# Routed experts of a perceiver block: GpSimd rounds with a one-tensor operation, VectorE waits later for split weights, and the last up product moves behind an output

## Chip, cores and metric

The kernel runs on one core of one Trainium2 chip. The metric is the device time of one execution in microseconds (us); the median of three runs stands for a kernel.

## The reference

The function takes `x` (16 x 64 tokens of 512 features) and a context (16 x 1601 x 512). It adds a cross attention over the context, then a relative-position self attention, then a block with latent attention and a mixture of experts. Only the last part is touched:

```
def moe(xn, Wg_s, Wu_s, Wd_s, Wg_r, Wu_r, Wd_r, W_router, routing_bias):
    shared = silu(xt @ Wg_s) * (xt @ Wu_s) @ Wd_s
    probs = jax.nn.sigmoid(xt @ W_router + routing_bias)
    scores, idx = jax.lax.top_k(probs, TOPK)             # TOPK = 2 of ER = 7
    scores = scores / jnp.sum(scores, axis=-1, keepdims=True)
    wts = jnp.sum(jax.nn.one_hot(idx, ER) * scores[..., None], axis=1)
    g = jnp.einsum('th,ehi->tei', xt, Wg_r)
    u = jnp.einsum('th,ehi->tei', xt, Wu_r)
    combined = jnp.einsum('tei,eih,te->th', silu(g) * u, Wd_r, wts)
    return shared + combined
```

All 1,024 tokens go to a shared expert and each to two of seven routed ones. Every weight matrix is 512 x 512, in float32.

## The kernel before

**Precision.** A float32 product is made of three products in the type fp32r: a number is split into a rounded part `hi` and the rest `lo`, and `x_lo*w_hi + x_hi*w_lo + x_hi*w_hi` are summed in one PSUM bank (`routed_product`, L1150 to L1152; four chunks of 128 features, so 12 matmuls of 128 x 512 for one product).

**Tiles.** The 2,048 pairs of token and expert are sorted by expert into slots of a table in memory. Each expert's pairs are filled up to whole tiles of 128 slots, 22 tiles at most; all 22 are computed, and those past the last pair belong to no token. The table `tile_expert` tells for each tile where its expert's weights lie (its ring place) and which expert's split it needs.

**The weights' ring.** There are seven routed experts and three ring places (`RING3`) with three matrices each (gate, up, down). SyncE loads a matrix into `ring_raw` (L564); expert e is loaded once TensorE has done the up products of the tiles of expert e-3, and its down matrix once their outputs are done. The split of the first expert is made by ScalarE and VectorE, and the `hi` part of the second by ScalarE. The rest is GpSimd's (loop over e, L1358 to L1366): for experts 3 to 7 it writes `ring_hi` as the sum of `ring_raw` and a zero column broadcast to the whole matrix (L1363), 15 times, and for experts 2 to 7 `ring_lo` as `ring_raw - ring_hi` (L1365), 18 times. After the third matrix of an expert it raises `split_ready`.

**One tile t, engine by engine.** The order on each engine is written out by hand.

- ScalarE: `load_rows(t+2)` starts the loads of a later tile's rows, `routed_silu(t)` makes silu of the gate product into `rhm`, `output_rows(t-1)` copies the output of the tile before (L1749) and stores it to `y_slots`, `hidden_columns_out(t)` rounds the turned hidden rows (L1743).
- VectorE: `rows_columns(t+1)` transposes the next tile's rows (L2466), writes their `hi` parts `xg_hi` in four pieces (L2470), waits for `split_ready` to reach the number that tile t+1 needs, and writes `xg_lo` in four pieces (L2476), the last of which raises `xgT_ready`. Then `routed_mult(t)` multiplies silu of gate by up into `rhm` (L2483), and `hidden_split(t)` writes the `lo` part of the turned hidden rows (L2488).
- TensorE: `routed_hidden(t)` first does `hidden_columns(t-1)`, four transposes of `rhm` (L1177) that wait for `routed_mult(t-1)`; then it waits for `xgT_ready` and does the gate and the up product of tile t. `routed_output(t-1)` is the down product of the tile before.

So a wait of TensorE for split weights is not its own: it is passed on by VectorE through `xgT_ready`.

**The end.** After tile 20's output would come tile 21's; the code before ends with gate(21), up(21), the transposes of tile 21, output(20), output(21). Tile 21 uses other buffers for its hidden parts (`rhm_last`, which are called xg_hi and xg_lo in the trace). GpSimd waits until the stores of all tiles that hold pairs have landed (L1372), and gathers rows of `y_slots` with 16 indirect DMAs (L1378), two for each block of 128 tokens; the ninth also waits for gate(21). VectorE adds gathered rows to `y` for six blocks (L2513, L2517), TensorE sums the blocks 4 and 5 behind output(21) (L1229, L1233), and SyncE and ScalarE store the results.

Of the kernel before, what the change touches and what calls it, by code (L numbers as in the profile page):

```python
# [15 lines left out]
ds = bass.ds  # L16
# [116 lines left out]
def perceiver_kernel(nc, x, ctx_keys, consts, vecs, rows, Wq, Wv, Wr, Wout, Wkvd, Wqd, Wku, Wqu, Wvu, Wropeq, Wropek,  # L133
                     Wo, Wexp, Wrouter, out):
    with ExitStack() as ctx:
# [438 lines left out]
        def _(pe):  # L574
# [577 lines left out]
                    last = nc.tensor.matmul(b[:], x_hi[:, c, :], hi, start=False, stop=c == HC - 1)  # L1152
                last.then_inc(full, 1)

            def routed_hidden(t, par, at):


                if not (isinstance(t, int) and t < 2):
                    hidden_columns(t - 1)
                pe.wait_ge(xgT_ready, t + 1)  # L1160
                for m, b, full in ((gate, 1, rgate_full), (up, 2, rup_full)):
                    if isinstance(t, int) and t == 0:
                        pe.wait_ge(down_added, NT - 2 if m == gate else NT - 1)
                    else:
                        pe.wait_ge(rsilu_ready if m == gate else rhm_ready, t)
                    routed_product(bank[b], m, at, xg_hi[par], xg_lo[par], full)
                    if isinstance(t, int) and t == 1 and m == gate:
                        hidden_columns(0)
# [51 lines left out]
                    routed_hidden(t, par, at[n + 1])  # L1220
                    routed_output(t - 1, 1 - par, at[n])
            at = places_of(TILES - 2, 2)
            routed_hidden(TILES - 1, 1, at[1])
            hidden_columns(TILES - 1)
            routed_output(TILES - 2, 0, at[0])
            routed_output(TILES - 1, 1, at[1])
            pe.wait_ge(gate_ready, 2)
            for n, k in enumerate(SUMMED):
# [8 lines left out]
        def _(pool):  # L1237
# [116 lines left out]

            pool.wait_ge(slots_ready, 5)
            pool.wait_ge(split_ready, 1)
            zero = cst[:, C_ZERO:C_ZERO + 1].unsqueeze(2).broadcast_to([P, HC, D])
            for e in range(1, NR):  # L1358
                for n, m in enumerate(order_of(e)):
                    pool.wait_ge(routed_loaded[m], 16 * (e + 1))  # L1360
                    at = (slice(None), PLACES[e], m)
                    if e > 1:
                        nc.gpsimd.tensor_tensor(ring_hi[at], ring_raw[at], zero, ALU.add).then_inc(split_hi, 1)  # L1363
                    pool.wait_ge(split_hi, 3 * e + n + 1)
                    last = nc.gpsimd.tensor_tensor(ring_lo[at], ring_raw[at], ring_hi.bitcast(F32)[at], ALU.subtract)  # L1365
                last.then_inc(split_ready, 1)  # L1366
# [35 lines left out]
        def _(act):  # L1402
# [367 lines left out]
            def routed_step(t, par, turn, load=True):  # L1770
                if load:
                    act.wait_ge(xgT_full, t + 1)
                    load_rows(t + 2, par)
                routed_silu(t)
                if isinstance(t, int) and t == TILES - 1:
                    hidden_columns_out(t)
                    output_rows(t - 1, 1 - par, turn)
                else:
                    output_rows(t - 1, 1 - par, turn)
                    hidden_columns_out(t)  # L1780

            act.wait_ge(slots_ready, 4)
            for n, k in enumerate(SUMMED):
# [18 lines left out]
        def _(dve):  # L1802
# [648 lines left out]
            def down_out(k):  # L2451
                dve.wait_ge(down_full, k + 1)
                dve.tensor_tensor(y[:, k, :], bank[k % 4][:], y[:, k, :], ALU.add).then_inc(down_added, 1)
# [4 lines left out]
                return dve.tensor_tensor(ring_lo[at], ring_raw[at], ring_hi.bitcast(F32)[at], ALU.subtract)  # L2458


            def rows_columns(t, par, turn):
                first = isinstance(t, int) and t == 0
                if not first:
                    nth = dve.value_load(tile_expert[0:1, 1, ds(t, 1)], min_val=1, max_val=NR)
                dve.wait_ge(xg_loaded[par], 64 * turn)
                dve.transpose(xgT[par].rearrange("p a (g q) -> p a g q", q=B32),  # L2466
                              xg[par].rearrange("p g (a e) -> p a g e", e=B32)).then_inc(xgT_full, 1)
                dve.wait_ge(xgT_full, t + 1)
                for c in range(HC):
                    last = dve.tensor_scalar(xg_hi[par][:, c, :], xgT[par][:, c, :], vec[:, V_W2B + c:V_W2B + c + 1], None, ALU.mult)  # L2470
                last.then_inc(xg_split, 1)
                dve.wait_ge(xg_split, t + 1)
                if not first:
                    dve.wait_ge(split_ready, nth)
                for c in range(HC):
                    last = dve.scalar_tensor_tensor(xg_lo[par][:, c, :], xgT[par][:, c, :], vec[:, V_W2B + c:V_W2B + c + 1],  # L2476
                                                    xg_hi[par].bitcast(F32)[:, c, :], ALU.mult, ALU.subtract)
                last.then_inc(xgT_ready, 1)

            def routed_mult(t):  # L2480
                dve.wait_ge(rup_full, t + 1)
# [9 lines left out]
            for k in range(NT - 2):  # L2491
                down_out(k)
                if k in (3, 4):
                    first_low(k - 3)
            rows_columns(0, 0, 1)
            down_out(NT - 2)
            first_low(2).then_inc(split_ready, 1)
            down_out(NT - 1)
            rows_columns(1, 1, 1)
            routed_mult(0)  # L2500
            hidden_split(0)
            with dve.Fori(0, TILES // 2 - 1) as i:
                for par in range(2):
                    t = 2 * i + 1 + par
                    rows_columns(t + 1, par, i + 2)
                    routed_mult(t)
                    hidden_split(t)
            routed_mult(TILES - 1)
            hidden_split(TILES - 1)
# [48 lines left out]
```

## Time and profile before

| | |
|---|---|
| median of 3 runs | 812.97 us (812.67 to 815.89) |
| the profiled execution | 810.25 us |
| its span in the trace | 808.4 us |
| TensorE busy | 767.6 us (95%) |
| VectorE busy | 530.5 us (66%) |
| ScalarE busy | 355.3 us (44%) |
| GpSimd busy | 301.0 us (37%) |
| mean granted TensorE clock | 0.989 |

In the trace, PE is TensorE, PEld its weight loads, DVE VectorE, ACT ScalarE, POOL GpSimd and SP SyncE; a q behind a name is the engine's queue of instructions that are not computing, such as those that start DMAs. Matmuls overlap in the records, so that their starts, not their durations, give the pace. A time in brackets behind an instruction is how long its engine was idle before it, with what ended that.

### The profile page before, as it was taken

What the parts mean: (1) busy time and instruction counts of PE and PEld (TensorE: products, weight loads), DVE (VectorE), ACT (ScalarE), POOL (GpSimd) and SP (SyncE); (2) the same over time, 40 slices, a digit from 0 to 9 for tenths busy, and PEclk for the clock granted to TensorE, in tenths of its full rate; (3) what the DMA queues carried; (4) which work ended last, traced back from release to release, by engine and by line L of the source; (5) the groups of instructions that cost most, each with busy time, mean ns of one, the idle gap of its engine ahead of it and who ended that gap; (6) DMA issues with size and microseconds to landing.
All of it is one profiled execution on the core that took longest, in us unless ns stands there. A gap on an engine that the chain in (4) does not pass through costs nothing.

```text
span 808.4 us, 17795 instructions
## 1 busy us (share of the span) xinstructions
PE 767.6 (95%) x6855; PEld 564.8 (70%) x6857; DVE 530.5 (66%) x1147; ACT 355.3 (44%) x913; POOL 301.0 (37%) x157
## 2 busy tenths in 40 slices
PE   4899999999899999999999999899999999997996
PEld 4554455554657778878877787677888888885884
DVE  5898797797644447676788888856475545544445
ACT  4356446562253428853258877723522122121221
POOL 1000000000431943643022222443639999994034
PEclk9999999999889999999999999999999999998999
DMA  9968666883511022040179000040658466531138
GB/s 342 386 254 304 209 245 233 318 318 125 223 33 74 0 60 101 2 127 12 52 270 384 25 0 1 2 157 2 228 179 296 135 209 200 184 111 45 52 116 274
DMA packets 56082, 127.08 MB, mean 157 GB/s; under 512 B 5057, under 2 KB 20673, under 8 KB 49873
## 3 DMA queue, kind: packets, MB, share of 16 engines
q1 hardware_dynamic: 36752, 105.44, 36.7%
q10 hardware_dynamic: 16704, 12.33, 4.8%
q0 software_dynamic: 2560, 8.39, 3.1%
q8 instruction: 48, 0.79, 0.4%
q14 instruction: 18, 0.14, 0.1%
HBM read 101.99 MB, written 24.15 MB: 156 GB/s over the span
## 4 chain that ended last, share of the span: by engine, by line
PE 61%; POOL 20%; DVE 8%; DMA 4%; ACT 3%; issue 3%; SPq 0%; POOLq 0%; DVEq 0%; ACTq 0%
PE scores L622 11%; PE bank L652 10%; POOL ring_lo L1365 10%; POOL ring_hi L1363 7%; DMA nat<-in_ctx_keys 3%; POOL picked L1378 2%; PE bank L702 2%; PE bank L856 2%; PE bank L703 2%; PE bank L857 2%; PE bank L862 2%; PE bank L704 2%; PE bank L1029 2%; PE bank L892 2%; PE bank L637 2%
## 5 line engine op out<-in xcount | busy, mean ns | idle before, releaser
L1845 DVE STREAM_TRANSPOSE ctxT<-nat 128x1024 f32<-128x1024 f32 (+3 forms) x124 | 116.8, 1003 | 8.5 <-DMA nat<-in_ctx_keys 8.2
L652 PE MATMUL bank<-nat,probT 128*64 128x512 f32 (+1 forms) x416 | 94.6, 601 | 0.1
L1365 POOL TENSOR_TENSOR ring_lo<-ring_raw,ring_hi 128x2048 fp32r<-128x2048 f32 x18 | 82.9, 4608 | 14.2 <-DVE ring_lo L2458 13.0
L1244 POOL TENSOR_TENSOR wq_lo<-wq_raw,wq_hi 128x1024 fp32r<-128x1024 f32 x4 | 9.3, 2357 | 210.4 <-ACT wq_hi L1476 210.4
L1150 PE MATMUL bank<-ring_hi,xg_lo 128*128 x180 | 72.7, 404 | 0.0
L1152 PE MATMUL bank<-ring_hi,xg_hi 128*128 x180 | 70.8, 393 | 0.0
L1151 PE MATMUL bank<-ring_lo,xg_hi 128*128 x180 | 70.6, 392 | 0.0
L652 PEld LDWEIGHTS bank<-nat,probT 128*64 128x64 f32 (+1 forms) x416 | 28.1, 137 | 52.0 <-issue 48.4
L2488 DVE TENSOR_TENSOR rhm_lo<-bank,rhm_hi 128x512 fp32r<-128x512 f32 x21 | 14.5, 692 | 73.0 <-ACT rhm_hi L1743 73.0
L622 PE MATMUL scores<-ctxT,hn 32*64 32x416 f32 (+8 forms) x1536 | 56.5, 427 | 5.1 <-issue 3.7
L622 PEld LDWEIGHTS scores<-ctxT,hn 32*64 32x64 f32 x1536 | 42.7, 131 | 21.3 <-issue 13.5
L1749 ACT COPY hn<-bank 128x512 f32<-128x512 f32 x22 | 12.9, 587 | 94.8 <-PE bank L1152 94.8
L1363 POOL TENSOR_TENSOR ring_hi<-ring_raw,cst 128x2048 fp32r<-128x2048 f32 x15 | 54.1, 3605 | 0.0
L1636 ACT ACTIVATE sp<-bank,s_bias 128x64 f32<-128x64 f32 x128 | 38.1, 327 | 19.0 <-DVE s_bias L2200 18.8
L1296 POOL TENSOR_TENSOR sp<-sp,s_inv 128x512 f32<-128x512 f32 x16 | 16.8, 1051 | 77.1 <-DVE s_inv L2206 77.1
L1152 PEld LDWEIGHTS bank<-ring_hi,xg_hi 128*128 128x128 f32 x180 | 34.1, 189 | 7.5
L1151 PEld LDWEIGHTS bank<-ring_lo,xg_hi 128*128 128x128 f32 x180 | 34.2, 190 | 6.7
L1150 PEld LDWEIGHTS bank<-ring_hi,xg_lo 128*128 128x128 f32 x180 | 34.3, 190 | 6.5
L622 PE MATMUL scores<-ctxT,qn 32*64 32x385 f32 (+5 forms) x960 | 34.6, 432 | 0.7 <-DVE ctxT L1845 0.7
L622 PEld LDWEIGHTS scores<-ctxT,qn 32*64 32x64 f32 x960 | 26.3, 131 | 10.7 <-issue 4.9
L1378 POOL DMA_INDIRECT picked<-y_slots,slots x16 | 16.0, 1000 | 46.7 <-POOLq L1372 42.1
L1150 PE MATMUL bank<-ring_hi,rhm_lo 128*128 x84 | 32.8, 390 | 0.0
(316 smaller groups left out, 1914.7 us busy)
## 6 DMA issues: line engine op xcount, KB each, us to landing
nat<-in_ctx_keys SPq DMA_DIRECT2D x48, 1024.0 KB, 8.9
ring_raw<-in_Wexp SPq DMA_DIRECT2D x21, 1024.0 KB, 6.1
x_slots<-zeros SPq DMA_DIRECT2D x1, 5632.0 KB, 18.2
y_slots<-zeros SPq DMA_DIRECT2D x1, 5632.0 KB, 32.6
hn<-x_slots ACTq DMA_DIRECT2D x88, 64.0 KB, 2.1
y_slots<-hn ACTq DMA_DIRECT2D x22, 256.0 KB, 4.2
w_raw<-in_Wexp SPq DMA_DIRECT2D x3, 1024.0 KB, 5.6
nat<-in_ctx_keys SPq DMA_DIRECT2D x16, 130.0 KB
```

The lines of the kernel that those rows point to most:

```text
L622: last = nc.tensor.matmul(scores4[64 * b:64 * b + 64, i, at], queries[rows_i, j, 64 * b:64 * b + 64], ctxT[rows_i, b, j, at], start=start, ...
L637: last = nc.tensor.transpose(prob_bank(k, f)[0:n, (j % 4) * P:(j % 4 + 1) * P], prob[:, j, 0:n], ident)
L652: last = nc.tensor.matmul(context_bank(k)[64 * b:64 * b + 64, :], probT[0:n, j, 64 * b:64 * b + 64], nat[k % 2][0:n, b, j, :], start=j == ...
L1150: nc.tensor.matmul(b[:], x_lo[:, c, :], hi, start=c == 0, stop=False)
L1151: nc.tensor.matmul(b[:], x_hi[:, c, :], lo, start=False, stop=False)
L1152: last = nc.tensor.matmul(b[:], x_hi[:, c, :], hi, start=False, stop=c == HC - 1)
L1296: nc.gpsimd.tensor_tensor(sp_[par][:, at, :], sp_[par][:, at, :], s_inv[par][:, at].unsqueeze(2).broadcast_to([P, 8, SQ]), ALU.mult).then_ ...
L1363: nc.gpsimd.tensor_tensor(ring_hi[at], ring_raw[at], zero, ALU.add).then_inc(split_hi, 1)
L1365: last = nc.gpsimd.tensor_tensor(ring_lo[at], ring_raw[at], ring_hi.bitcast(F32)[at], ALU.subtract)
L1378: nc.gpsimd.indirect_dma_start(picked[2 * k + i][:], None, y_slots, bass.IndirectOffsetOnAxis(slots[:, k, i:i + 1], 0)).then_inc(picked_lo ...
L1636: last = nc.scalar.activation(sp_[par][:, h, :], bank[4 + f][:, n * SQ:(n + 1) * SQ], ACT.Exp, bias=s_bias[par][:, h:h + 1], scale=SELF_SCALE,
L1845: dve.transpose(dst, src).then_inc(columns_ready, 1)
```

## The change

Three edits. (1) GpSimd's `ring_hi` of experts 3 to 7 is written by a `tensor_scalar` that adds the constant 0.0 instead of a `tensor_tensor` that adds a broadcast column. (2) VectorE writes three pieces of `xg_lo(t+1)`, then the product `routed_mult(t)`, and only then waits for `split_ready` and writes the fourth piece (`rows_end`); the lookup of the number is a function `need_of`. (3) On TensorE, output(20) comes between gate(21) and up(21), and the transposes of tile 21 behind up(21); ScalarE's order in the last tile follows.

```diff
-            def routed_hidden(t, par, at):
-                if not (isinstance(t, int) and t < 2):
-                    hidden_columns(t - 1)
-                pe.wait_ge(xgT_ready, t + 1)
-                for m, b, full in ((gate, 1, rgate_full), (up, 2, rup_full)):
+            def routed_hidden(t, par, at, which=None):
+                which = which or (gate, up)
+                if gate in which:
+                    if not (isinstance(t, int) and t < 2):
+                        hidden_columns(t - 1)
+                    pe.wait_ge(xgT_ready, t + 1)
+                for m in which:
+                    b, full = (1, rgate_full) if m == gate else (2, rup_full)
...
-            routed_hidden(TILES - 1, 1, at[1])
+            routed_hidden(TILES - 1, 1, at[1], (gate,))
+            routed_output(TILES - 2, 0, at[0])
+            routed_hidden(TILES - 1, 1, at[1], (up,))
             hidden_columns(TILES - 1)
-            routed_output(TILES - 2, 0, at[0])
             routed_output(TILES - 1, 1, at[1])
...
-            zero = cst[:, C_ZERO:C_ZERO + 1].unsqueeze(2).broadcast_to([P, HC, D])
...
-                        nc.gpsimd.tensor_tensor(ring_hi[at], ring_raw[at], zero, ALU.add).then_inc(split_hi, 1)
+                        nc.gpsimd.tensor_scalar(ring_hi[at], ring_raw[at], 0.0, None, ALU.add).then_inc(split_hi, 1)
...
-                if isinstance(t, int) and t == TILES - 1:
-                    hidden_columns_out(t)
-                    output_rows(t - 1, 1 - par, turn)
-                else:
-                    output_rows(t - 1, 1 - par, turn)
-                    hidden_columns_out(t)
+                output_rows(t - 1, 1 - par, turn)
+                hidden_columns_out(t)
...
+            def need_of(t):
+                return dve.value_load(tile_expert[0:1, 1, ds(t, 1)], min_val=1, max_val=NR)
+
             def rows_columns(t, par, turn):
-                first = isinstance(t, int) and t == 0
-                if not first:
-                    nth = dve.value_load(tile_expert[0:1, 1, ds(t, 1)], min_val=1, max_val=NR)
...
-                if not first:
+                for c in range(HC - 1):
+                    rows_low(par, c)
+
+            def rows_low(par, c):
+                return dve.scalar_tensor_tensor(xg_lo[par][:, c, :], xgT[par][:, c, :], vec[:, V_W2B + c:V_W2B + c + 1],
+                                                xg_hi[par].bitcast(F32)[:, c, :], ALU.mult, ALU.subtract)
+
+            def rows_end(par, nth=None):
+
+                if nth is not None:
                     dve.wait_ge(split_ready, nth)
-                for c in range(HC):
-                    last = dve.scalar_tensor_tensor(xg_lo[par][:, c, :], xgT[par][:, c, :], vec[:, V_W2B + c:V_W2B + c + 1],
-                                                    xg_hi[par].bitcast(F32)[:, c, :], ALU.mult, ALU.subtract)
-                last.then_inc(xgT_ready, 1)
+                rows_low(par, HC - 1).then_inc(xgT_ready, 1)
...
             rows_columns(0, 0, 1)
+            rows_end(0)
...
             rows_columns(1, 1, 1)
+            rows_end(1, need_of(1))
             routed_mult(0)
             hidden_split(0)
             with dve.Fori(0, TILES // 2 - 1) as i:
                 for par in range(2):
                     t = 2 * i + 1 + par
+                    nth = need_of(t + 1)
                     rows_columns(t + 1, par, i + 2)
                     routed_mult(t)
+                    rows_end(par, nth)
                     hidden_split(t)
```

## Rows read from the trace of the kernel before

**Rows 1.** The waits, 600 to 809 us: in total, times, longest (us).

```profile
DVE y L2513 <- DMA picked<-y_slots,slots: 3.5, 1, 3.5
PE bank L1177 <- DVE rhm L2483: 6.2, 2, 5.4
```

**Rows 2.** Table of stretches: busy time (instructions) by engine, clock, DMA share, GB/s.

```profile
733.90:739.50 5.60, 0.18 (x2) 0.01 (x1) 1.72 (x5) 0.58 (x1) 3.72 (x1) 0.69 0.12 47
739.50:743.00 3.50, 3.50 (x11) 2.94 (x12) 1.63 (x3) 0.59 (x1) 0.00 (x0) 0.51 0.13 37
```

**Rows 3.** Order of time, ScalarE's output copies of tiles: start, duration (us).

```profile
734.19 0.58 ACT L1749 COPY hn<-bank 128x512 f32<-128x512 f32 x1 [4.84 <-PE bank L1152]
...
750.03 0.59 ACT L1749 COPY hn<-bank 128x512 f32<-128x512 f32 x1 [4.92 <-PE bank L1152]
...
758.68 0.59 ACT L1749 COPY hn<-bank 128x512 f32<-128x512 f32 x1 [4.85 <-PE bank L1152]
...
797.41 0.58 ACT L1749 COPY hn<-bank 128x512 f32<-128x512 f32 x1 [2.14 <-PE bank L1152]
```

**Rows 4.** Order of time on GpSimd, VectorE and TensorE around 735 us.

```profile
733.11 4.51 POOL L1365 TENSOR_TENSOR ring_lo<-ring_raw,ring_hi 128x2048 fp32r<-128x2048 f32 x1
...
737.72 1.12 DVE L2476 SCALAR_TENSOR_TENSOR xg_lo<-bank,vec,xg_hi 128x128 fp32r<-128x128 f32 x4 [7.25 <-POOL ring_lo L1365]
...
733.69 0.39 PE L1152 MATMUL bank<-ring_hi,rhm_hi 128*128 x1
739.50 1.11 PE L1177 MATMUL bank<-cst,rhm 128*128 128x128 f32 x4 [5.42 <-DVE rhm L2483]
740.26 0.78 PE L1150 MATMUL bank<-ring_hi,xg_lo 128*128 x1
...
742.95 0.39 PE L1150 MATMUL bank<-ring_hi,xg_lo 128*128 x1
```

**Rows 5.** Groups by form on GpSimd: count, busy us, mean ns of one, idle.

```profile
L1365 POOL TENSOR_TENSOR ring_lo<-ring_raw,ring_hi 128x2048 fp32r<-128x2048 f32 x18 | 82.9, 4608 | 14.2 <-DVE ring_lo L2458 13.0
L1363 POOL TENSOR_TENSOR ring_hi<-ring_raw,cst 128x2048 fp32r<-128x2048 f32 x15 | 54.1, 3605 | 0.0
...
L1289 POOL MEMSET kT_h<- 128x2048 f32 x2 | 3.6, 1814 | 4.7 <-ACT o_hi L1586 4.7
```

**Rows 6.** Loads of the last expert's matrices on SyncE, and all 18 loads' landing.

```profile
696.80 0.92 SPq L564 DMA_DIRECT2D ring_raw<-in_Wexp  x2
...
708.17 0.37 SPq L564 DMA_DIRECT2D ring_raw<-in_Wexp  x1
...
DMA to landing us min/median/max: 5.4/6.0/11.9
```

**Rows 7.** Order of time in an ordinary tile, VectorE and TensorE.

```profile
636.28 0.69 DVE L2483 TENSOR_TENSOR rhm<-rhm,bank 128x512 f32<-128x512 f32 x1 [0.42 <-PE bank L1152]
...
638.81 0.60 PE L1177 MATMUL bank<-cst,rhm 128*128 128x128 f32 x4
639.16 0.48 PE L1150 MATMUL bank<-ring_hi,xg_lo 128*128 x1
```

**Rows 8.** The chain that ended last, its tail: start, duration (us), what.

```profile
776.73 2.09 DMA y_slots<-hn
...
779.72 0.99 POOL picked L1378
...
799.34 5.90 DMA picked<-y_slots,slots
```

**Rows 9.** Order of time in tile 21, TensorE and VectorE.

```profile
791.21 0.66 PE L1177 MATMUL bank<-cst,rhm 128*128 128x128 f32 x4 [0.78 <-DVE rhm L2483]
...
792.52 0.69 DVE L2488 TENSOR_TENSOR xg_lo<-bank,xg_hi 128x512 fp32r<-128x512 f32 x1 [1.37 <-ACT xg_hi L1743]
```

**Rows 10.** Table of stretches in the tail, columns as in the second group.

```profile
792.00:796.00 4.00, 4.00 (x19) 3.29 (x18) 3.41 (x5) 1.07 (x2) 3.12 (x3) 1.00 0.76 195
...
800.00:804.00 4.00, 2.85 (x7) 0.95 (x5) 1.42 (x2) 1.17 (x2) 0.29 (x1) 1.00 1.00 369
```

## The prediction

> **What bounds the kernel now.** I read the page first, then the waits, the table of stretches, and the orders of time of TensorE, GpSimd, VectorE and ScalarE around the one hole that they show.
>
> The chain makes GpSimd look like the bound of the routed stage: its 33 splits of weights are 137 us of work almost without a pause [rows 5]. The waits say otherwise: from 600 us to the end TensorE's products waited only 6.2 us for another engine, in two waits, and 5.4 of them are one wait for rhm of VectorE [rows 1]. The table of stretches shows it: in 733.90 to 739.50 TensorE is busy for 0.18 us of 5.60, and then runs a stretch at a granted clock of 0.51, the lower of its two levels, 1.2 GHz [rows 2]. So TensorE sets the pace, and GpSimd matters only where its result comes late, which happens once.
>
> Which tile this is follows from ScalarE's copies of outputs. There are 22, one for each tile, and seven come after the one at 734.19; that one is tile 14 and the next, at 750.03, is tile 15 [rows 3]. TensorE's order is hidden(t), output(t-1), so it stood after output(14), ahead of hidden(16). Its first step there is hidden_columns(15), which needs rhm(15) from routed_mult(15). On VectorE that stands behind rows_columns(16), which waits for the seventh expert's split. The order of time reads: the last ring_lo ends at 737.62, the four xg_lo (VectorE had waited 7.25 us for them) start at 737.72, rhm follows, and the transposes start at 739.50 [rows 4]. TensorE waited for a product whose inputs had long been there.
>
> The price of the hole: the copies of tiles 14 and 15 are 15.84 us apart, those of 15 and 16 8.65 [rows 3], so 7.2 us are lost. By parts: the stand from 733.92 to 739.50 is 5.58; the four transposes took 0.76 to the next product's start, where 0.35 is usual (638.81 to 639.16); six products began over 740.26 to 742.95, 2.69 us, where six steps of 0.23 take 1.4 (a period of 8.65 less 0.35 holds 36 products), so 1.3 more [rows 3, 4, 7]. The sum is 7.3.
>
> **Part 1, the rounding on GpSimd.** 15 instructions of 3.60 us (128x2048, one full operand and a broadcast column) become 15 with one tensor operand; the 18 subtractions of 4.61 stay [rows 5]. Call the new price T. The trace holds no one-tensor operation on GpSimd. Bounds: 1.81 us, a memset of the same size, which only writes; above, 4.61, two full operands. A gain below 1.81 is excluded, since as many elements are written. Nearest is the 3.60 row, the same reads and writes but for the broadcast column, and the step from 4.61 to 3.60 shows that a lighter second operand is cheaper; with none I take 2.2, between the memset and that row, and keep both ends.
>
> How small must T be? Without a hole gate(16) would begin at 733.92 (the last product's start, 733.69, and a step) plus 0.35 for the transposes, 734.3 [rows 4]. With the new order of VectorE (part 2) it can begin some 0.5 us after the last subtraction: 0.1 for the signal (737.62 to 737.72), some 0.3 for one xg_lo (four take 1.12 [rows 4]), and 0.1 for TensorE to see it. So the last subtraction must end by 733.8 instead of 737.62: 3.8 us in 15 instructions, 0.25 each, T at most 3.35. At 2.2 GpSimd has 21 us less work, if nothing else stops it.
>
> The loads do stop it then, harmlessly. The two first matrices of the last expert are issued at 696.80 and the third at 708.17, landing in a median 6.0 us [rows 6]; with T = 2.2 GpSimd handles a matrix in 6.9, so it ends at about 714.2 + 6.9, or 702.8 + 3 x 6.9 = 723.5. With the longest landing, 11.9, the third arrives at 720.1 and ends at 727. Both lie ahead of 733.8. These loads wait for TensorE's tiles, which keep their times up to the hole. Nothing else queues behind GpSimd until the gathers, which start after tile 18's store (part 3).
>
> The rows have 3.60 us for the broadcast form and 1.81 for the memset [rows 5], and none for a one-tensor operation. By the Trainium skill, GPSIMD Engine Reference, section 3.1, a light body with one input is bound by its port at 1.03 cycles an element and a two-input one at about 2.6; at the page's 1.2 GHz that makes an estimate of 1.76 us for T and 4.4 for both old forms. The row of 3.60 does not agree with the second; no row here shows the first, and the saving would be the same 7.2 us by it.
>
> **Part 2, the wait behind the product.** VectorE now does transpose, four xg_hi, three xg_lo, rhm, the wait, one xg_lo. Nothing is added but order. What the moved xg_lo costs when no wait bites: rhm at 636.28 to 636.97 follows up(t)'s end, and one xg_lo, 0.3 (four take 1.12 [rows 4]), ends at 637.4; TensorE reaches the transposes at 638.81, after the output [rows 7]. So 1.4 us of cover, zero cost in each tile. Queued behind the wait is hidden_split, needed only after a further gate and up product. Tile 1's table lookup moves from ahead of its transpose to between its third and last xg_lo, once, where it can delay that piece by less than one piece costs; I put 0 to 0.3 us there, taking 0. Alone, this part lets gate(16) begin at 737.62 + 0.5 = 738.1 instead of 740.26: 2.1 us.
>
> Parts 1 and 2 together close the hole: 7.2 us, not their sum, as both pay for the same stand.
>
> **Part 3, the last up product behind an output.** GpSimd's gathers were freed by the store of the last used tile: they begin at 779.72, once the store that began at 776.73 has landed, and that is tile 18's, four copies after tile 14's; the later tiles hold no pairs [rows 3, 8]. So the earlier output(20) gains nothing. gate(21), which the ninth gather needs, stays where it is. The loss: before, output(20) covered ScalarE's cast and VectorE's subtraction of tile 21. Now TensorE goes from up(21) to transposes (which wait for rhm, as now), and then has nothing while cast and subtraction run. From the start of the transposes to the end of tile 21's xg_lo is 791.21 to 793.21, 2.0 us [rows 9], of which 0.4 is transposing: 1.6 us of new stand. Everything on TensorE after it, the sums of token blocks 4 and 5, slips by 1.6. On VectorE the sums of the other blocks, which follow that xg_lo, start 2.7 later (a whole product, 12 steps of 0.23).
>
> What of that reaches the end? The last store follows the last gather's landing; VectorE waited 3.5 us for a gather in the tail [rows 1], more than the 2.7. But the out stores move later into a DMA system that is full: its share is 0.76 in 792 to 796 and 1.00 in 800 to 804 [rows 10], and the last gather took 5.90 us to land there [rows 8]. About 1 us of idle share from 792 to 796 can no longer be used. So 0 to 2.7 us; I take 1.0.
>
> **Sum.** 7.2 - 1.0 = 6.2 us. The profiled span of 808.4 becomes 802.2; that execution's own time, 810.25, becomes 804.0. The runs' median is 812.97, 2.7 above it; the difference applies there too: 806.8 us.
>
> **Rivals.**
> - *The broadcast column was free.* T is 3.35 to 3.94. For it: an add of a constant may cost the same loop. Against it: 4.61 against 3.60. At T = 3.60 only part 2 pays: -2.1 + 1.0, 811.9 us.
> - *The slower side.* The scalar form is a costlier routine on GpSimd than the two-tensor add. The seventh expert's weights then come so late that TensorE's hole outgrows the old one: at 4.61 the last split ends 15.1 us later, gate(16) with it, so +15.1 - 2.1 + 1.0 = +14.0, 827 us. Break-even is T = 3.67, and 0.5% slower is reached at 3.94. For it: no row shows the form. Against it: it reads less.
> - *The tail takes it back.* With the full 2.7, 812.97 - 7.2 + 2.7 = 808.5. Within the forecast's own range, since nothing suggests more.
>
> **Numbers.** Forecast (T under 3.35) 0.80; by the tail's two ends it gives 805.8 to 808.5, and with 1.5 us below and 0.5 above for scatter (the three runs before lie 3.2 apart) its own range is 804.3 to 809.0. Broadcast free 0.09; slower routine 0.10; something else, mostly a worse tail, 0.01. 0.5% of 812.97 is 4.1 us, about what a measurement can tell from no change. The forecast lies under 808.9: faster 0.80. The free column gives no difference, 0.10. Slower 0.10. The range takes in the forecast and the free column and leaves the slower routine out: 804.3 to 812.3.
>
> **What would show it.** GpSimd's one-tensor rows under 3.35 us (2.2 expected), with pauses for loads in the last two experts; no stand of TensorE and no fall of its clock before tile 16; copies of outputs every 8.65 us; a stand of about 1.6 us after tile 21's transposes; gathers from 772.5. Wrong would be: a form above 3.35 us; a stand of gate(t) behind the moved xg_lo in ordinary tiles, 21 times; a tail in which the last gather lands later than 25.5 us after the first gather's start.

## The result: slower by 3.8%

The changed kernel took 843.9 us (median of 4 runs, 843.3 to 845.6) against 812.8 for the kernel before (4 runs, 811.0 to 815.9). The ratio is 1.038, 95% interval 1.035 to 1.042: 31 us slower, where 6.2 us faster was forecast. The profiled execution took 843.75 us with a span of 841.7, 33.3 more than the span before. In all ratios here a run that took over 1.5% longer than the fastest of its kernel is left out; it was one in all, of changed_again below.

Groups by form on GpSimd from 560 us on, the changed kernel (answers to [rows 5]; count, busy us, mean ns of one, idle):

```profile
L1368 POOL TENSOR_TENSOR ring_lo<-ring_raw,ring_hi 128x2048 fp32r<-128x2048 f32 x18 | 82.6, 4593 | 14.8 <-DVE ring_lo L2457 13.6
L1366 POOL TENSOR_SCALAR ring_hi<-ring_raw 128x2048 fp32r<-128x2048 f32 x15 | 80.6, 5373 | 0.0
```

The form with one tensor operand takes 5.37 us, above the 3.60 that it replaces and above the subtraction with two full operands. The subtraction is unchanged. GpSimd has 15 x 1.77 = 26.5 us more to do, and its last split ends at 761.58, where it ended at 737.62 [rows 4].

Waits of the changed kernel, 590 to 842 us (answers to [rows 1]):

```profile
DVE xg_lo L2476 <- POOL ring_lo L1368: 32.2, 4, 11.9
...
PE bank L1150 <- DVE xg_lo L2476: 24.8, 5, 10.1
...
DVE rhm L2488 <- remote: 15.5, 1, 15.5
...
ACT hn L1752 <- remote: 12.0, 1, 12.0
...
PE bank L1180 <- DVE rhm L2488: 10.0, 1, 10.0
```

VectorE now waits for GpSimd four times, and TensorE behind it. The wait has moved as the second edit meant it to: TensorE's waits for split weights stand at L1150, the gate product, and no longer at the transposes. New against the trace of before are waits for a "remote" releaser, which is the profile's word for one that it can't name.

Order of time, ScalarE's output copies in the changed kernel (answers to [rows 3]; tiles 7 to 20, those left out are a period apart):

```profile
670.90 0.58 ACT L1752 COPY hn<-bank 128x512 f32<-128x512 f32 x1 [4.54 <-PE bank L1152]
680.76 0.59 ACT L1752 COPY hn<-bank 128x512 f32<-128x512 f32 x1 [4.92 <-PE bank L1152]
...
698.06 0.58 ACT L1752 COPY hn<-bank 128x512 f32<-128x512 f32 x1 [4.84 <-PE bank L1152]
713.13 0.59 ACT L1752 COPY hn<-bank 128x512 f32<-128x512 f32 x1 [4.94 <-PE bank L1152]
721.78 0.58 ACT L1752 COPY hn<-bank 128x512 f32<-128x512 f32 x1 [4.30 <-PE bank L1152]
743.47 0.59 ACT L1752 COPY hn<-bank 128x512 f32<-128x512 f32 x1 [5.19 <-PE bank L1152]
752.12 0.58 ACT L1752 COPY hn<-bank 128x512 f32<-128x512 f32 x1 [4.84 <-PE bank L1152]
772.15 0.59 ACT L1752 COPY hn<-bank 128x512 f32<-128x512 f32 x1 [4.92 <-PE bank L1152]
...
806.66 0.59 ACT L1752 COPY hn<-bank 128x512 f32<-128x512 f32 x1 [4.84 <-issue]
824.38 0.59 ACT L1752 COPY hn<-bank 128x512 f32<-128x512 f32 x1 [12.04 <-remote]
```

Subtract the period of 8.65 us from each of the four long steps, and 1.2, 6.4, 13.0 and 11.4 are left: four holes of 32.0 us in all, where there was one of 7.2. TensorE's longest stands, in its order of time:

```profile
702.19 0.79 PE L1150 MATMUL bank<-ring_hi,xg_lo 128*128 x1 [3.81 <-DVE xg_lo L2476]
732.16 0.79 PE L1150 MATMUL bank<-ring_hi,xg_lo 128*128 x1 [10.06 <-DVE xg_lo L2476]
762.11 0.79 PE L1150 MATMUL bank<-ring_hi,xg_lo 128*128 x1 [9.67 <-DVE xg_lo L2476]
```

Each stands in front of a gate product. The last one is gate(16), 21.9 us later than the 740.26 of before [rows 4]. GpSimd's splits had begun 2.6 us earlier than before in this execution (597.61 against 600.20), so the routed stage itself has lost 24.4 us.

The stretches show what comes with a long stand (busy us by engine, clock, DMA share, GB/s, as in [rows 2]):

```profile
721.00:742.00 21.00, 10.94 (x38) 8.59 (x38) 4.52 (x12) 1.77 (x3) 20.83 (x6) 0.67 0.08 25
742.00:752.00 10.00, 10.00 (x48) 8.22 (x48) 4.10 (x10) 1.77 (x3) 9.92 (x3) 1.00 0.17 52
752.00:771.00 19.00, 9.33 (x38) 7.47 (x36) 4.52 (x12) 1.77 (x3) 9.50 (x2) 0.73 0.09 28
```

GpSimd is busy without a pause until its last split ends at 761.58, while TensorE stands for half of the two long stretches. The clock falls from 1.00 to a mean of 0.67 and 0.73, that is, part of these stretches runs at 1.2 GHz: behind the stand that ends at 762.11 the products first begin 0.43 us apart, and from 765.52 on 0.23.

The rest of the 33.3 us is in the tail. The order of time on all engines there, with most rows left out:

```profile
801.84 1.05 POOL L1381 DMA_INDIRECT picked<-y_slots,slots  x1 [40.26 <-POOLq L1375]
...
811.74 0.60 ACT L1742 ACTIVATE rhm<-bank 128x512 f32<-128x512 f32 x1 [3.46 <-remote]
...
814.42 0.39 PE L1150 MATMUL bank<-ring_hi,xg_lo 128*128 x1
...
820.72 0.95 POOL L1381 DMA_INDIRECT picked<-y_slots,slots  x1 [0.30 <-issue]
...
824.38 0.59 ACT L1752 COPY hn<-bank 128x512 f32<-128x512 f32 x1 [12.04 <-remote]
824.50 0.69 DVE L2488 TENSOR_TENSOR rhm<-rhm,bank 128x512 f32<-128x512 f32 x1 [15.50 <-remote]
```

up(21) has its last product near 815, yet VectorE goes on at 824.50, and ScalarE, whose next work is the copy of output(20), at 824.38. Output(20) had been through TensorE by 812.4. By the code VectorE waits there for up(21) and for ScalarE's silu, which had ended at 812.34, and ScalarE for output(20); so it looks as if TensorE's signals came late, though the profile names no releaser. Both go on together, after the last gather was issued at 820.72 and after the DMA engines had gone quiet, at 823.9. From the first gather to the end the tail takes 841.7 - 801.84 = 39.9 us, where it took 808.4 - 779.72 = 28.7 [rows 8]. So 33.3 is made of 24.4 + 0.3 + 11.2 - 2.6. The 0.3 is lost behind gate(16)'s start, where the low clock lasts longer: eight steps from product to product take 3.41 us, and took 3.14 before. The experiments had to tell whether the routed stage's loss and the tail's are both the change's.

### The profile page after: what moved, and what is told of

It is laid out like the page before. It is cut to its first block, busy times and chain, and to the rows that moved or that the text cites. A ratio compares the mean times of both kernels' runs of the same rounds, so it can differ in the third digit from the quotient of the medians.

```text
span 841.7 us, 17777 instructions
## 1 busy us (share of the span) xinstructions
PE 773.0 (92%) x6856; PEld 567.9 (67%) x6857; DVE 531.2 (63%) x1147; ACT 355.3 (42%) x913; POOL 326.9 (39%) x157
## 4 chain that ended last, share of the span: by engine, by line
PE 62%; POOL 20%; DVE 7%; DMA 3%; ACT 3%; issue 3%; another core or an unknown queue 1%; SPq 0%; POOLq 0%; ACTq 0%; DVEq 0%
PE scores L622 10%; PE bank L652 10%; POOL ring_hi L1366 10%; POOL ring_lo L1368 9%; DMA nat<-in_ctx_keys 3%; PE bank L702 2%; PE bank L1150 2%; PE bank L856 2%; PE bank L704 2%; PE bank L862 2%; PE bank L857 2%; PE bank L703 2%; PE bank L1152 2%; PE bank L1151 2%; PE bank L637 2%
## 5 line engine op out<-in xcount | busy, mean ns | idle before, releaser
L1150 PE MATMUL bank<-ring_hi,xg_lo 128*128 x180 | 76.6, 425 | 26.3 <-DVE xg_lo L2476 24.8
L1366 POOL TENSOR_SCALAR ring_hi<-ring_raw 128x2048 fp32r<-128x2048 f32 x15 | 80.6, 5373 | 0.0
L1152 PE MATMUL bank<-ring_hi,xg_hi 128*128 x180 | 73.6, 409 | 0.0
L1151 PE MATMUL bank<-ring_lo,xg_hi 128*128 x180 | 73.5, 408 | 0.0
L1150 PEld LDWEIGHTS bank<-ring_hi,xg_lo 128*128 128x128 f32 x180 | 36.1, 200 | 34.9 <-issue 28.0
L2476 DVE SCALAR_TENSOR_TENSOR xg_lo<-bank,vec,xg_hi 128x128 fp32r<-128x128 f32 x88 | 26.6, 345 | 33.0 <-POOL ring_lo L1368 32.2
L1152 PEld LDWEIGHTS bank<-ring_hi,xg_hi 128*128 128x128 f32 x180 | 35.9, 199 | 8.4
L1742 ACT ACTIVATE rhm<-bank 128x512 f32<-128x512 f32 x22 | 13.2, 598 | 66.4 <-PE bank L1152 53.9
L1151 PEld LDWEIGHTS bank<-ring_lo,xg_hi 128*128 128x128 f32 x180 | 36.2, 201 | 7.1
L2488 DVE TENSOR_TENSOR rhm<-rhm,bank 128x512 f32<-128x512 f32 x22 | 15.1, 685 | 32.6 <-PE bank L1152 17.0
L622 PE MATMUL scores<-ctxT,qn 32*64 32x385 f32 (+6 forms) x960 | 34.8, 432 | 0.5 <-issue 0.5
```

What stands on the lines that cost most here:

```text
L622: last = nc.tensor.matmul(scores4[64 * b:64 * b + 64, i, at], queries[rows_i, j, 64 * b:64 * b + 64], ctxT[rows_i, b, j, at], start=start, ...
L1150: nc.tensor.matmul(b[:], x_lo[:, c, :], hi, start=c == 0, stop=False)
L1151: nc.tensor.matmul(b[:], x_hi[:, c, :], lo, start=False, stop=False)
L1366: nc.gpsimd.tensor_scalar(ring_hi[at], ring_raw[at], 0.0, None, ALU.add).then_inc(split_hi, 1)
L2476: return dve.scalar_tensor_tensor(xg_lo[par][:, c, :], xgT[par][:, c, :], vec[:, V_W2B + c:V_W2B + c + 1], xg_hi[par].bitcast(F32)[:, c, : ...
```

## Experiments

All ratios are against the kernel before, run beside the kernel on the same chip, with 95% intervals; us are the ratio's part of that kernel's median. There were four groups of runs, each on one chip: the first four experiments; changed_again to copy_rounding; copy_only to before_traced; and the last four, on the chip of the first group.

| run | rounding | VectorE's order | tail's order | ratio (interval) | us |
|---|---|---|---|---|---|
| changed (the result) | scalar | new | new | 1.038 (1.035 to 1.042) | +31 |
| only_rounding | scalar | old | old | 1.033 (1.029 to 1.037) | +26.4 |
| only_vector | broadcast | new | old | 0.997 (0.995 to 0.999) | -2.3 |
| only_tail | broadcast | old | new | 1.0005 (0.9986 to 1.0023) | +0.4 |
| no_rounding | broadcast | new | new | 0.998 (0.996 to 1.000) | -1.9 |
| changed_again | scalar | new | new | 1.029 (1.025 to 1.032) | +23.1 |
| no_tail | scalar | new | old | 1.029 (1.026 to 1.032) | +23.6 |
| late_tail | broadcast + memset | new | new | 1.030 (1.027 to 1.032) | +23.9 |
| copy_rounding | copy | new | old | 0.991 (0.988 to 0.994) | -7.4 |
| copy_only | copy | old | old | 0.992 (0.989 to 0.995) | -6.7 |
| copy_all | copy | new | new | 0.991 (0.988 to 0.994) | -7.1 |
| scalar_times | scalar, times 1.0 | old | old | one run | +33 |
| before_traced | broadcast | old | old | one run | +1 |
| changed_third | scalar | new | new | 1.034 (1.030 to 1.038) | +27.7 |
| rounding_again | scalar | old | old | 1.032 (1.028 to 1.036) | +26.4 |
| late_again | broadcast + memset | new | new | 1.030 (1.024 to 1.035) | +24.1 |
| changed_apart | scalar | new | new, gathers later | 1.039 (1.035 to 1.043) | +31.8 |

### Each edit alone, and the change without the first

**only_rounding.** The first edit of the diff and nothing else.

```diff
-                        nc.gpsimd.tensor_tensor(ring_hi[at], ring_raw[at], zero, ALU.add).then_inc(split_hi, 1)
+                        nc.gpsimd.tensor_scalar(ring_hi[at], ring_raw[at], 0.0, None, ALU.add).then_inc(split_hi, 1)
```

> The kernel before with the first edit alone: GpSimd's 15 roundings as an add of a constant. The changed kernel shows 5.37 us for one. Theory A (two causes: a dearer routine, and the tail's order by itself): the last split ends 15 x (5.37 - 3.60) = 26.6 us later; in the old order of VectorE the whole of it reaches TensorE, so +26 to +27 us, and the tail from the first gather to the end keeps its 28.7 us. Theory B (one cause: the long stand in the tail comes with the scalar form, through the late seventh expert or through what the form leaves on GpSimd): the tail is 38 to 40 us here too, +37 us in all.

Measured: +26.4 us, 5.37 us for one, and a tail of 30.0 us (836.8 - 806.83): theory A. This is the first edit's price, 15 x 1.77 = 26.5. TensorE's waits are in the old place and larger:

```profile
DVE xg_lo L2475 <- POOL ring_lo L1364: 34.5, 5, 12.7
...
PE bank L1177 <- DVE rhm L2482: 27.7, 5, 10.9
```

**only_vector.** The second edit alone (in part; the whole of it stands in the diff of the change).

```diff
+                for c in range(HC - 1):
+                    rows_low(par, c)
...
                     dve.wait_ge(split_ready, nth)
-                for c in range(HC):
-                    last = dve.scalar_tensor_tensor(xg_lo[par][:, c, :], xgT[par][:, c, :], vec[:, V_W2B + c:V_W2B + c + 1],
-                                                    xg_hi[par].bitcast(F32)[:, c, :], ALU.mult, ALU.subtract)
-                last.then_inc(xgT_ready, 1)
+                rows_low(par, HC - 1).then_inc(xgT_ready, 1)
...
                     rows_columns(t + 1, par, i + 2)
                     routed_mult(t)
+                    rows_end(par, nth)
```

> The kernel before with the second edit alone: the last xg_lo behind the product. Both theories: the same last split, 2.1 us less of a stand before tile 16, no cost elsewhere: -2 us, tail 28.7 us. A rival that the moved piece costs time in each tile would show periods above 8.65 us and a gain below 0.

Measured: -2.3 us, interval -4.0 to -0.7. In TensorE's waits a row at the gate product has taken the place of the old 5.4 us at the transposes [rows 1]:

```profile
DVE xg_lo L2480 <- POOL ring_lo L1368: 5.7, 1, 5.7
...
PE bank L1150 <- DVE xg_lo L2480: 3.7, 1, 3.7
```

Counted from GpSimd's first split, gate(16) begins after 137.95 us (597.89 to 735.84), where it took 140.06 (600.20 to 740.26): 2.1 us earlier, as expected. The copies of tiles 14 and 15 are 14.20 us apart, so the hole shrank only from 7.2 to 5.6. Most of the difference is the clock: ten steps from product to product behind the stand take 3.97 us, and took 3.60 before.

**only_tail.** The third edit alone.

```diff
-            routed_hidden(TILES - 1, 1, at[1])
-            hidden_columns(TILES - 1)
+            routed_hidden(TILES - 1, 1, at[1], (gate,))
             routed_output(TILES - 2, 0, at[0])
+            routed_hidden(TILES - 1, 1, at[1], (up,))
+            hidden_columns(TILES - 1)
             routed_output(TILES - 1, 1, at[1])
```

> The kernel before with the third edit alone: output(20) between gate(21) and up(21). Theory A: the tail from the first gather to the end grows from 28.7 to near 40 us as in the changed kernel, +10 to +11 us, and ScalarE's copy of output(20) waits for the end of all gathers. Theory B: no long stand, the tail grows by 0 to 2.7 us, about 1 as the prediction had it.

Measured: +0.4 us with an interval of -1.1 to +1.9, so nothing that can be told. The new stand behind the transposes is there, and it is off the path:

```profile
791.42 0.66 PE L1180 MATMUL bank<-cst,rhm 128*128 128x128 f32 x4 [0.78 <-DVE rhm L2483]
793.56 0.49 PE L1150 MATMUL bank<-ring_hi,xg_lo 128*128 x1 [1.49 <-DVE xg_lo L2488]
```

The traced tail is 806.6 - 777.20 = 29.4 us instead of 28.7. Theory A, that the tail's order by itself brings the long stand, falls.

**no_rounding.** The changed kernel with the rounding of before.

> The changed kernel with the first edit undone: the rounding is again a sum with a broadcast column, the other two edits stand. Theory A: the sum of its two parts, -2 + 11 = +9 us against the kernel before. Theory B: -2 + 1 = -1 us.

Measured: -1.9 us, interval -3.5 to -0.2. The three edits add up (26.4 - 2.3 + 0.4 = 24.5), but to 6 or 7 less than the 31 of the first result.

### The change again, late by other means, and another one-tensor form

**changed_again.** The changed kernel, unchanged, beside the next three on another chip.

> The changed kernel once more, beside the others on one chip, for the long stand in its tail (10 us on TensorE after up(21), ScalarE and VectorE idle until the last gather has landed). The four runs so far show no part but the rounding that costs time, and rounding, VectorE's order and tail add up to +25.5 us, the changed kernel to +31. Theory A (the stand is the two edits' doing together): it comes again, +30 to +32 us. Theory B (it came by chance in that program's load or chip): +25 to +26 us, and the tail from the first gather is 29 to 30 us.

Measured: +23.1 us, and a traced tail of 830.4 - 800.29 = 30.1 us. So the program doesn't always have the long stand. One of its four runs took 848.14 us, where the others took 832 to 835; it was not traced, and its +36 us lie above even theory A's range. The tail is as theory B had it, and the time of the three other runs 2 us under its range.

**no_tail.** The changed kernel with the tail's old order.

> The changed kernel with the third edit undone. Both theories: +27.8 - 2.3 = +25.5 us. Theory A adds that it has no long stand after up(21), the changed kernel of the same call does. If it has one too, the tail's order has no part in it.

Measured: +23.6 us, where 25.5 was expected, and within 0.5 us of changed_again. The traced tail is 833.7 - 803.12 = 30.6 us. As neither trace has the long stand, the pair can't tell whether the tail's order has a part in it.

**late_tail.** no_rounding, with a memset and a wait for it ahead of each rounding:

```diff
+                        nc.gpsimd.memset(ring_hi.bitcast(F32)[at], 0.0).then_inc(pos_cleared, 1)
+                        pool.wait_ge(pos_cleared, 3 * (e - 2) + n + 2)
                         nc.gpsimd.tensor_tensor(ring_hi[at], ring_raw[at], zero, ALU.add).then_inc(split_hi, 1)
```

> The kernel with the second and third edit and the old rounding (no_rounding), made late by other means: ahead of each of the 15 roundings GpSimd fills the same tile with a memset of 1.81 us, and waits for it, so that rounding takes 5.4 to 5.5 us as in the changed kernel without the scalar form. Theory C (the stand hangs on the lateness and the tail's order): a stand of some 10 us after up(21), +30 to +33 us. Theory D (it hangs on the scalar form itself, or on nothing but chance): no stand, +25 to +28 us.

Measured: +23.9 us. Its rounding costs 3.60 and 1.81, and a short wait, 5.49 in all:

```profile
L1369 POOL TENSOR_TENSOR ring_hi<-ring_raw,cst 128x2048 fp32r<-128x2048 f32 x15 | 54.0, 3602 | 1.2
L1367 POOL MEMSET ring_hi<- 128x2048 f32 x15 | 27.2, 1811 | 0.0
```

The traced tail is 836.1 - 804.62 = 31.5 us, without the long stand, so theory C does not hold for this run. The same lateness from other instructions costs the same time. So what the scalar form costs is its duration; it need not disturb another engine to explain the loss.

**copy_rounding.** only_vector with a copy that changes the type on its way:

```diff
-                        nc.gpsimd.tensor_tensor(ring_hi[at], ring_raw[at], zero, ALU.add).then_inc(split_hi, 1)
+                        nc.gpsimd.tensor_copy(ring_hi[at], ring_raw[at]).then_inc(split_hi, 1)
```

> The kernel with the second edit (only_vector) and a one-tensor form of another kind: a copy with the type changed on the way instead of the sum. Theory E (one tensor read is what makes a form cheap on GpSimd, and the scalar form's 5.37 us is its own): 1.8 to 2.5 us for one, the last split ends before 730 us, no stand of TensorE before tile 16, -7 us. Theory F (any one-tensor form runs the slow routine): 5.4 us, +25 us.

Measured: -7.4 us, the gain that the prediction promised for the hole (7.2). The groups:

```profile
L1367 POOL TENSOR_TENSOR ring_lo<-ring_raw,ring_hi 128x2048 fp32r<-128x2048 f32 x18 | 83.0, 4616 | 15.0 <-DVE ring_lo L2460 13.8
L1365 POOL CAST ring_hi<-ring_raw 128x2048 fp32r<-128x2048 f32 x15 | 28.5, 1899 | 9.8 <-DMA ring_raw<-in_Wexp 9.8
```

and GpSimd's order of time in the last expert:

```profile
700.61 1.90 POOL L1365 CAST ring_hi<-ring_raw 128x2048 fp32r<-128x2048 f32 x1 [6.37 <-DMA ring_raw<-in_Wexp]
...
715.63 4.62 POOL L1367 TENSOR_TENSOR ring_lo<-ring_raw,ring_hi 128x2048 fp32r<-128x2048 f32 x1
```

The copy takes 1.90 us, GpSimd waits for loads in the last two experts (9.8 us in two), and its last split ends at 720.3, before the 733.8 of the prediction. Theory E holds. TensorE has no hole (15.00 of 15.00 us busy, at a clock of 1.00), and the copies of tiles 14 and 15 are 8.65 us apart (732.38 and 741.03):

```profile
715.00:730.00 15.00, 15.00 (x71) 12.45 (x70) 8.20 (x21) 3.54 (x6) 5.18 (x2) 1.00 0.22 70
730.00:745.00 15.00, 15.00 (x71) 12.39 (x71) 6.48 (x16) 3.54 (x6) 0.00 (x0) 1.00 0.21 66
```

### What is worth keeping, and whose price 5.37 us is

**copy_only** is the kernel before with this copy alone, **copy_all** has all three edits with the copy.

> The kernel before with the rounding as a type-changing copy and nothing else; VectorE's order and the tail are the old ones. Theory: the hole before tile 16 is one sum of 7.2 us that either a quicker rounding or nothing closes, and with 1.9 us for one the wait's place no longer matters. So -7 to -8 us, the same as copy_rounding within 0.3%. Rival: the moved piece of xg_lo gives something by itself beside the hole, so that copy_only is 2 us behind copy_rounding, -5 to -6.

> All three edits with the copy in place of the scalar form. By the prediction's sum -7.2 + 1.0 = -6.2 us; by what only_tail measured (+0.1, no cost) -7 to -8 us.

Measured: -6.7 us (interval -8.9 to -4.5) and -7.1 (-9.5 to -4.7). The two and copy_rounding can't be told from each other. By these times alone the rival's 2 us can't be excluded; the traces decide. In copy_only, as in copy_rounding, the copies of tiles 14 and 15 are 8.65 us apart (732.48 and 741.13), so the hole is gone in the old order of VectorE too, and TensorE waits 0.3 us for xg_lo in all where copy_rounding waits 0.4. Once no split is late, neither the wait's place nor the tail's order gives or costs a measurable time. All three beat the kernel before by 0.8 to 0.9%, and the changed kernel by more.

**scalar_times**, only_rounding with another operation:

```diff
-                        nc.gpsimd.tensor_scalar(ring_hi[at], ring_raw[at], 0.0, None, ALU.add).then_inc(split_hi, 1)
+                        nc.gpsimd.tensor_scalar(ring_hi[at], ring_raw[at], 1.0, None, ALU.mult).then_inc(split_hi, 1)
```

> One look: the kernel before with the scalar form as a product with 1.0 instead of a sum with 0.0. If the scalar form is one routine whatever its operation, 5.37 us for one and a span near that of only_rounding (+26 us). If it is the addition that is slow, near 1.9 us and a span some 7 us under the kernel before.

```profile
L1362 POOL TENSOR_SCALAR ring_hi<-ring_raw 128x2048 fp32r<-128x2048 f32 x15 | 80.5, 5369 | 0.0
...
DVE rhm L2482 <- remote: 11.4, 1, 11.4
```

A product costs what a sum costs. The price is the scalar form's, for both operations. The span was 840.9, with an unnamed wait of VectorE of 11.4 us in the tail's old order: a tail of 840.9 - 804.97 = 35.9 us.

**before_traced**, the kernel before beside it:

> One look: the kernel before unchanged, to have its tail traced beside the others of this call. If the waits for an unknown releaser in the tail belong to the changed order or the lateness, it has none. If they belong to the chip, it has them where the others of the call have them.

```profile
ACT rhm L1739 <- remote: 5.1, 1, 5.1
```

It has an unnamed wait on ScalarE of 5.1 us, and GpSimd one of 2.0 at the ninth gather; its tail is 810.0 - 778.74 = 31.3 us. So a small form of these waits comes without any of the three edits. All traces of the second group and of this one have it, ScalarE's wait for gate(21) at 5 us and GpSimd's at 2 (copy_only has a further one of ScalarE, 4.7), but for scalar_times, which has the long form. None of the four traces of the first group has an unnamed wait in the tail. So whether there is one went by the group here, not by the kernel.

### The stand in the tail

Four more kernels ran on the first group's chip, six runs each. **changed_apart** is the changed kernel with one more wait:

```diff
             for k in range(NT):
+                if k == 0:
+                    pool.wait_ge(rup_full, TILES)
```

> The changed kernel, for the scatter of its times beside the other three. Without the long stand in the tail +22 to +25 us on the kernel before of the same chip, with it +31 to +36. If the stand comes by the run, the times fall in two groups; if by the chip, in one.

> only_rounding once more (scalar form, old orders). If the tail's order brings the stand, none above +29 us; if the scalar form or lateness does, as many runs with +33 to +38 as in changed_third.

> late_tail once more (late by memsets, no scalar form, new orders). If the lateness brings the stand, as many runs with +31 or more as in changed_third; if the scalar form does, none, all at +23 to +26.

> The changed kernel with GpSimd's first gather waiting for the last up product, some 12 us later than now. If the gathers hold TensorE's signals back, gate(21), output(20) and up(21) signal within 0.5 us of their last product, no ScalarE or VectorE wait of over 5 us in the tail beside the gathers' own landing, and no run stands apart from the others: the changed kernel without the stand + 10 to 12 us in each. If they have no part in it, the stand comes here too, in some runs.

Measured, all runs in us: changed_third 842.7 to 849.0; rounding_again 840.3 to 843.6; late_again 836.2 to 839.0 in four runs and 843.8 and 845.4 in two; changed_apart 846.2 to 850.6. The kernel before took 812.1 to 821.1, a median 8 us above that of the first group (808.5), on the same chip. Tails by the traces: 846.5 - 806.38 = 40.1, 838.3 - 803.29 = 35.0, and 836.0 - 805.50 = 30.5 us.

The times did not fall as the expectations had them. Five runs of changed_third lie at +26 to +29 us, between the two groups that were expected, and one at +32; rounding_again has no run above +29, by which the tail's order would have been the cause, yet its trace shows the stand; late_again lies at +20 to +22 in four runs and +27 and +29 in two. With the kernel before itself 8 us up and scattered over 9, these marks could not decide, and what follows rests on the traces, one for each kernel.

In the traces of the two that have the scalar form and overlapping gathers the stand is there, in the new order and in the old:

```profile
DVE rhm L2488 <- remote: 15.6, 1, 15.6
```

```profile
DVE rhm L2482 <- remote: 8.4, 1, 8.4
```

(the first is changed_third, the second rounding_again). late_again has only the small form, 4.9 us on ScalarE. In rounding_again the releases are these:

```profile
818.89 0.69 DVE L2482 TENSOR_TENSOR rhm<-rhm,bank 128x512 f32<-128x512 f32 x1 [8.44 <-remote]
...
822.22 0.95 POOL L1377 DMA_INDIRECT picked<-y_slots,slots  x1 [0.30 <-issue]
...
825.22 0.59 ACT L1742 CAST xg_hi<-bank 128x512 fp32r<-128x512 f32 x1 [11.39 <-remote]
```

VectorE went on at 818.89, 5 us after up(21)'s last product and before the last gather was even issued (822.22). So not all of these waits last until the gathers have landed, as the first trace suggested.

changed_apart has no wait for an unnamed releaser. Its gathers start after the last up product. The 54.8 us are GpSimd's added wait, ScalarE's seven waits for output products are the ordinary ones of each tile, and TensorE waits for a gather:

```profile
POOL picked L1383 <- PE bank L1152: 54.8, 1, 54.8
ACT hn L1754 <- PE bank L1152: 30.0, 7, 4.9
...
PE bank L1237 <- DMA picked<-y_slots,slots: 13.3, 1, 13.3
```

So the stand was seen only where TensorE and gathers overlap, and not in each run that has the overlap: only_rounding, traced on the same chip, had a tail of 30.0 us, the same program as rounding_again 35.0. That the overlap is needed rests on the one trace of changed_apart, and on its six runs, which lie close together. The tail's order is not needed for the stand, since rounding_again and scalar_times have it in the old order. But it makes the stand dearer: with the new order the two tails are 39.9 and 40.1 us, with the old 35.9 and 35.0, and TensorE stands for 10.0 and 10.1 us against 8.6 and 5.6. Keeping gathers and TensorE apart costs more than it saves: +31.8 us, against +27.7 for changed_third. The median of changed_apart is 10.8 us above that of late_again's four shorter runs (848.6 and 837.8), about what the later start was expected to cost.

All four traces with the long stand have the scalar form, and three others with it (only_rounding, changed_again, no_tail) do not have the stand. Why it is seen with that form and not in the trace of late_again (two runs of six are long, and none of these was traced) is open, and so is what the engines wait for.

## Why the prediction was wrong

**The step that failed is the price T.** The text had "Nearest is the 3.60 row", took 2.2 and put an upper bound of 4.61 on it. The form measured 5.37, above both ends. The reasoning counted operands: what reads less can't cost more than what reads two tensors. But the two one-tensor forms differ by a factor of 2.8: copy 1.90, scalar 5.37. The price goes by the form of the instruction, and what in the form makes it is not shown. The memset row, taken as a mere floor, turned out to be near the copy, and no row is near the scalar form. The 10% for "a costlier routine" was named with its place and its threshold (3.94), but its price was tied to 4.61; at 5.37 its own sum gives 26.5 - 2.1 + 1.0 = +25.4, in place of the +14.0 given. The kernels with this price whose traced tail has no long stand measured +23.1 to +26.4.

By the Trainium skill, GPSIMD Engine Reference, section 3.1, T would have been an estimate of 1.76 us. For the copy the trace comes near it (1.90), for the scalar form it disagrees (5.37), and the measurement decides.

**The rule from T to time was right.** With T = 5.37 the last split ends 26.5 us later and gate(16) 2.1 less: 24.4. The trace has 24.4, and only_rounding, in the old order, 26.4. With T = 3.60 it gives -2.1 (only_vector: -2.3), and with T = 1.90 -7.2 (copy_rounding: -7.4, copy_only: -6.7). GpSimd's end under a quick form was put at 723.5 by the loads; with the copy's 1.90, and the loads issued 1.8 us earlier in that execution (694.99), the same sum gives 720.5, and it was 720.3.

**Part 2** was right on gate(16), 2.1 us earlier in only_vector's trace, and in its price of nothing: the periods of ordinary tiles are still 8.65 us. The sum took the low clock behind the stand as unchanged; it lasted longer, and the hole shrank by 1.6. That parts 1 and 2 pay for the same hole holds, too: its 7.2 us are gone in the traces of copy_only and of copy_rounding.

**Part 3** was right on TensorE (a new stand of 1.6 forecast, 1.49 measured). Its 1.0 us on the end can't be told from what was measured, +0.4 with an interval of -1.1 to +1.9 and a traced tail 0.7 us longer.

**Not foreseen** is the stand in the tail. It made some 6 of the first result's 31 us by the medians (31 less 24.5 for the three edits), and the tail of its traced run is 11.2 us longer than that of before. The step that left it out is the path: the text had the last store follow the last gather's landing. That landed 22 us after the first gather's start, within the 25.5 that the prediction gave as a sign, while the end followed TensorE's late last products and the sums behind them. The stand does not come from the third edit, which only makes it longer; what brings it is open.

The forecast of the sign hung on one unknown price with an 80% chance. The hole, its parts and the rule from T to time were right, and the forecast still missed by 37 us: 31.6 by the price of T and the rest by the tail.

## What to carry to other kernels

Don't price a form of an elementwise instruction by the number of its operands: measure the form once before it goes on an engine that is near its limit. Where a chain of equal instructions is late by a little, a price error of one is multiplied by their number and arrives in full (15 x 1.77 us here); so work out the price at which the sign turns, and ask what row stands near it. Going faster has an end that going slower lacks: with part 2, 0.25 us apiece would have closed the hole by the prediction's sum, and the copy, 1.70 us apiece cheaper, gained no more than the hole's 7.2. To round float32 weights to fp32r on GpSimd, a type-changing copy was the cheapest of the forms tried.

## What the runs showed of the hardware

- GpSimd, 128 x 2048 float32: memset 1.81 us, copy to fp32r 1.90, sum with a broadcast column 3.60, difference of two tensors 4.61, scalar sum or product 5.37.
- In some runs ScalarE, VectorE and GpSimd waited for TensorE's last products longer than its records explain, while indirect gathers ran. In the changed kernel output(20) was through by 812.4 and ScalarE went on at 824.38, 12 us later, up(21) near 815 and VectorE at 824.50. There both went on after the gathers had landed; in rounding_again VectorE did so before the last gather was issued (818.89 against 822.22). In the one trace with the gathers started later there was no such wait. That TensorE's signals are what came late is read from the code's waits and not shown, and the cause is not settled.
